# A tile's product with the values one step later in the two causal attentions of a decoder kernel

## The reference, cut to what matters

```python
scores = scale * einsum('bhqd,bhkd->bhqk', q, k)      # 2048 x 2048
scores = where(tril, scores, -inf)
out = einsum('bhqk,bhkd->bhqd', softmax(scores), v)
out = concat_heads(out) @ Wo.T + bo
x = layernorm(x + out)
```

## Time and profile before

| | |
|---|---|
| median of 3 runs | 2865.86 us (2857.93 to 2866.38) |
| the profiled execution | 2858.85 us |
| its span, first to last instruction | 2857.1 us |
| TensorE busy | 2657.4 us, 93% |
| VectorE busy | 2143.4 us, 75% |
| ScalarE busy | 1802.5 us, 63% |
| GpSimd busy | 533.8 us, 19% |
| mean granted TensorE clock | 0.963 |

### The profile page before, as it was taken

How to read it: one execution, slowest core, us unless ns; L and a number is a source line. 1 busy time by engine, 2 the same in 40 slices (tenths; PEclk the granted TensorE clock), 3 DMA queues, 4 the chain that set the end, 5 groups by cost and what they waited for, 6 DMA issues and landing times. The chain is left out here.

```text
span 2857.1 us, 93546 instructions
## 1 busy us (share of the span) xinstructions
PE 2657.4 (93%) x39187; PEld 1001.4 (35%) x39187; DVE 2143.4 (75%) x5870; ACT 1802.5 (63%) x2158; POOL 533.8 (19%) x742
## 2 busy tenths in 40 slices
PE   4999999999999999948999998999999999999997
PEld 1623333432222222324222224662222222266664
DVE  7689999479999999485899994139999999551115
ACT  2288888627777777733888886233888888822222
POOL 0078782030000000002222113212000000003330
PEclk8899999979999999978999999997999999999999
DMA  3456652241111110202111112010122221121112
GB/s 101 123 116 158 140 130 75 71 150 26 28 28 27 27 29 18 74 13 88 40 43 43 44 47 89 0 65 26 46 64 56 56 57 35 39 95 39 44 44 89
DMA packets 122804, 177.27 MB, mean 62 GB/s; under 512 B 38835, under 2 KB 89918, under 8 KB 122128
## 3 DMA queue, kind: packets, MB, share of 16 engines
q1 hardware_dynamic: 103344, 124.55, 16.5%
q0 software_dynamic: 13568, 46.17, 5.9%
q10 hardware_dynamic: 5472, 0.56, 0.2%
HBM read 131.75 MB, written 31.96 MB: 57 GB/s over the span
## 5 line engine op out<-in xcount | busy, mean ns | idle before, releaser
L811 DVE TENSOR_REDUCE mpart<-ps 128x1 f32<-128x512 f32 x1536 | 978.9, 683 | 77.2 <-PE ps L598 73.8
L598 PE MATMUL ps<-stack 48*32 48x512 f16 (+4 forms) x13312 | 939.5, 349 | 41.6 <-DVE mpart L811 12.8
L523 ACT ACTIVATE xT<-ps,exp_scale 128x1024 f32<-128x1024 f32 (+3 forms) x800 | 785.1, 1028 | 215.6 <-PE ps L619 107.0
L523 ACT ACTIVATE cn<-ps,exp_scale 128x1024 f32<-128x1024 f32 (+4 forms) x800 | 733.2, 959 | 155.2 <-PE ps L619 73.8
L619 PE MATMUL ps<-stack 50*32 50x512 f16 (+3 forms) x11648 | 761.3, 371 | 32.2 <-ACT xT L523 24.3
L598 PEld LDWEIGHTS ps<-stack 48*32 48x32 f16 x13312 | 276.5, 90 | 986.4 <-DVE mpart L811 515.1
L804 DVE CUSTOM_DVE_ANT_0 scrap<-ps,arena 128x512 bf16<-128x512 f32 x768 | 490.1, 686 | 40.7 <-PE ps L598 37.3
L668 PE MATMUL ps<-xT,vall 128*17 128x512 f32 (+4 forms) x3648 | 412.5, 512 | 2.6 <-POOL xT L482 1.7
L668 PE MATMUL ps<-cn,vall 128*17 128x512 f32 (+3 forms) x3392 | 408.4, 501 | 1.2 <-ACT cn L523 1.0
L619 PEld LDWEIGHTS ps<-stack 50*32 50x32 f16 x11648 | 202.2, 90 | 190.9 <-ACT xT L523 96.0
L788 DVE CUSTOM_DVE_ANT_0 scrap<-ps,scrap 128x128 bf16<-128x128 f32 (+3 forms) x512 | 247.3, 484 | 14.3 <-PE ps L598 8.9
(11 more groups left out here) (293 smaller groups left out, 2778.9 us busy)
## 6 DMA issues: line engine op xcount, KB each, us to landing
stack<-q_parts SPq DMA_DIRECT2D x384, 64.0 KB, 3.2
stack<-k_parts SPq DMA_DIRECT2D x192, 64.0 KB, 3.3
wbuf<-in_maskT POOLq DMA_DIRECT2D x48, 256.0 KB, 4.7
arena<-in_moe_w SPq DMA_DIRECT2D x19, 512.0 KB, 4.8
stack<-k_parts SPq DMA_DIRECT2D x192, 50.0 KB, 2.4
stack<-sums_inverse SPq DMA_DIRECT2D x16, 512.0 KB, 6.0
parts<-osb SPq DMA_DIRECT2D x240, 32.0 KB
wbuf<-in_mask POOLq DMA_DIRECT2D x16, 401.0 KB, 4.3
```

What stands on the lines that cost most here:

```text
L523: nc.scalar.activation(e.prob[tile % P_SLOTS][0:rows, half * HALF + first:(half + 1) * HALF], S_PS(g)[0:rows, first:HALF], ACT.Exp, scale= ...
L598: last = nc.tensor.matmul(bank[quarter(j), i * w:i * w + w], qs[b][rows, at:at + 32], ks[b][rows, a:a + w], start=True, stop=True)
L811: nc.vector.tensor_reduce(dst, src, AX, ALU.max).then_inc(unit_used, 1)
```

## The change

In the causal attentions the product of the tile that is complete with slot n moves from step n to step n+1, behind that step's scores and first units; the product of a head's last tile moves into step 0 of the next head, and that of the very last tile behind the loop. ScalarE's copy of the last head's output moves from behind the exponential of slot 1 to behind that of slot 2. The cross-attentions keep their order. No instruction is added or removed.

```diff
@@ units and slots
-    wide = not causal
+    wide, late_product = not causal, causal
@@ ScalarE, behind the exponential
-                        if n == 1 and h:
+                        if n == (2 if late_product else 1) and h:
                             copy_out(h - 1)
@@ TensorE, in step n of head h, behind the scores and the first units
-                        if slots[n][5]:
+                        if not late_product and slots[n][5]:
                             product(h, n)
+                        elif late_product and n and slots[n - 1][5]:
+                            product(h, n - 1)
+                        elif late_product and n == 0 and h:
+                            product(h - 1, ns - 1)
                         for u in now[middle:]:
                             unit(turned, u)
+                if late_product:
+                    product(H - 1, ns - 1)
                 pe.wait_ge(o_weights_in, 16 * NC)
```

## The result

The change made the kernel slower. The median of four runs is 2907.99 us (2906.55 to 2915.11) against 2861.89 us (2856.52 to 2866.38) in four runs of the kernel before: ratio 1.0175, with a 95% interval of 1.0161 to 1.0188. (The two profiled executions give 1.0175 too, the two medians alone 1.0161.) The profiled execution took 2908.75 us with a span of 2907.0 us, 49.9 more than the span before, at the same mean clock (0.962 against 0.963). The prediction said 2912.0.

The account below looks back on a forecast made before the run. VectorE was taken to set the pace in steps 1 to about 15, TensorE from 16 to the next head's step 0. 14.5 x (1.65 + 1.83) = 50.5 us on 2858.85 gave 2909, taken as 2912; range 2868 to 2937.

Parts of the forecast that it names:

- The ring of three banks: Steps 2 to 12: VectorE's three queued units run out before the next after a product (1.90 us); net 1.0 per head.
- overlap of 0.09: On VectorE, one maximum overlaps the next by 0.09 us, so lateness of 0.36 is printed as 0.27 idle.
- The sum per head: Middle and end of a causal head together: 1.65 us more in layer 0, 1.83 in layer 1.
- The total: Both causal attentions: 14.5 heads x (1.65 + 1.83) = 50.5 us more, nearly all on the path setting the end.
- The bounds: Loss over both causal stages: at least 18 us from the surest terms (1.2 per pair of heads), at most 66.
- absorbed case: VectorE's 1.5 us idle at the head boundary takes up the middle's added idle: no change, say 2863 us; chance 0.13.
- The end of a head: Slots 15 to 21 replace 16 to 22 before the next head's scores: 0.44 us, plus about 0.2 in layer 0.
- ScalarE's 0.3 in layer 1: Tile 5's product delays slot 15's scores, whose exponential releases slot 17's; ScalarE has 0.32 idle, needs some 0.6: 0.3 more.
- Before the exponentials of slots 6, 8, 10 and 12 ScalarE no longer waits.: Sign in even steps: scores no longer stand behind a product (0.52 at slot 12); said to give nothing.
- The copy: Step 2: done 0.1 to 0.4 us before tile 0's product may start; bound -0 to +0.3 per head.
- Balance: TensorE reaches products before the ring is full, VectorE's queue covers 1.90: about 0.9 us per head faster, 2833; chance 0.11.
- Half: The middle costs as worked out, but TensorE recovers 0.44 and 0.3: 33 us slower, 2892; within the 0.76 for slower.

Follow-up runs that it names:

- the end alone late: The kernel before with only the products of slots 16 to 23 one step late, copy in its old place: 1.0014.
- the mended kernels: Units 27, 31, 35 two places later: in the kernel after, 1.0095; in the kernel before with products 1-13, 20-23 and copy late, 1.0032.

## Why the prediction was right

Direction, size and the main mechanism were right. Two smaller statements, on ScalarE and on the copy, and one of the sums for the bounds were wrong; that the total fits to 0.8 us is in part luck.

- **The ring of three banks.** The prediction worked out a need of 1.90 us against VectorE's queue. In layer 0 it gave a lateness of 0.47, 0.36 and 0.46 in steps 4, 6 and 8, which by its own overlap of 0.09 would be printed as 0.38, 0.27 and 0.37: measured 0.41, 0.27 and 0.37. In step 12 it gave 0.2 (0.11 printed): 0.26 before unit 3 in the head shown; other heads have between 0 and 0.26 there, some with 0.24 to 0.30 before unit 6 instead. For layer 1 it gave 0.47, 0.60 and 0.25 in steps 6, 8 and 10, printed 0.38, 0.51 and 0.16: measured 0.41, 0.50 and 0.16. The ties of 0.10 to 0.12 in step 2 and in layer 1's step 4 are not printed. Turning the order of the units alone took away half of the loss (1.0175 to 1.0095) or made a similar one in the old kernel (1.0074), so this is shown, not only argued.
- **The sum per head.** From the second to the fifteenth turning of the maxima there are 13 heads. They run from 161.9 to 479.3 us in layer 0 before and from 161.7 to 500.0 after, in layer 1 from 1380.7 to 1694.6 and from 1405.7 to 1743.0. A head grows from 24.42 to 26.02 us in layer 0, 1.60 where 1.65 was predicted, and from 24.15 to 25.95 in layer 1, 1.80 where 1.83 was predicted. In the most regular heads of layer 0 it is only 1.49 (24.36 to 25.85); the kernel after has several longer ones, of 26.0 to 26.3 us, among them those with the idle before unit 6. The head's end is 0.57 of the predicted 0.64, which leaves 1.0 for the middle, as predicted.
- **The total.** Predicted were 50.5 us, 3.48 for each of 14.5 pairs of heads; measured were 22.7 and 27.0, 49.7 together. The 13 heads in between carry 44.2 of them. The first and the last interval grew by 0.6 and 1.3 us in layer 0 and by 2.4 and 1.2 in layer 1, 5.5 together, where the sum has 1.5 pairs of heads, 5.2. The prediction had no reason for this size at the edges of a stage, so that they fit is luck.
- **The bounds.** The lower one was added up wrongly: 0.47 + 0.36 - 0.6 + 0.44 is 0.67 and 0.47 + 0.60 - 0.5 + 0.44 is 1.01, so 1.7 per pair of heads and 24 us, and not 1.2 and 18. The range's lower end was taken from the absorbed case and doesn't hang on it.
- **The end of a head.** Predicted: tile 7's product in, tile 14's out, 0.44, and 0.2 for unit 9's wait. Measured: 0.35 up to the scores of slot 20 and 0.22 behind them. The 0.22 is the exchange of product widths and is there by itself with the end alone late. The 0.35 comes with the product of tile 7. A free step 16 gives nothing back (2.26 before, and 2.26 with the end alone late), so it starts from what was already a wait. How the 0.35 divides between the product's length and the 0.23 that the scores of slot 18 wait for ScalarE isn't shown.
- **ScalarE's 0.3 in layer 1.** Predicted as the exponential of slot 15 releasing the scores of slot 17; VectorE's idle of 0.33 before unit 2 is there. In the mended kernels it is 0.64, and it goes once the products of slots 11 and 13 come in their own steps. Right.
- **"Before the exponentials of slots 6, 8, 10 and 12 ScalarE no longer waits."** True, but not the whole: its waits moved to the odd slots, with 0.59 to 0.81 at slots 7, 9, 11 and 15, and the conclusion that this side is free was wrong. With the ring mended, scores that wait for exponentials are a part of what is left in 1.0118 (units late too), 1.0095 and 1.0032. The step of the working that failed, though the forecast didn't hang on it, is to take ScalarE's waits as idle time of an engine that isn't the bound: units stand behind scores on TensorE, so a late exponential is a late unit.
- **The copy.** Priced at -0 to +0.3 with "done before the product may start". As placed by the change it costs nothing visible. But the two halves of the edit aren't independent: a late copy with early products costs 1.1% and an early copy with late products adds 0.5%, of which about two thirds and somewhat under half stand in heads at full clock.
- **The rivals.** Absorbed: the idle at the head's end (0.51 and 0.99; 1.49) is unchanged to 0.01 us, so it takes up nothing. Balance: VectorE's queue doesn't cover the product. Half: the end of the head gives back nothing. The clock has hardly a part in it: the stretches shown have 1.00, and the mean is 1.00 from 150 to 500 us and 0.99 from 1370 to 1730 us.

Four comparisons put the parts side by side: the last four products late, -0.53%; the four before them late, +0.67% (1.0014 against 0.9947); the first seven late with the units mended, +0.85% (1.0032 against 0.9947); the narrow units in the product's queue, +0.80% (1.0175 against 1.0095). Together +1.79%, measured 1.75%. They were taken on several chips and need not add up, and slot 15's product by itself wasn't tried. But the traces say the same in us per head, between the turnings of the maxima as above: -0.29, +0.53, +0.38 and +0.98 in layer 0, together 1.60 (measured 1.60), and -0.45, +0.68, +0.84 and +0.74 in layer 1, together 1.81 (measured 1.80). No large part is missing.

## What to carry to other kernels

When an in-order engine feeds another through a small ring of buffers, a long operation on it belongs where the consumer's queue is longest in time, not in number: add up the durations of the buffers ahead and compare them with the wait, the operation and the start of the next one. An order of feeding work that looks arbitrary (which of the tiles is the narrow one) can then be worth as much as the place of the operation. And when moving something one step, divide the move: here the same edit was a gain for the last four products, which puts one product less ahead of the next head's first scores, and a loss in each other group that was tried. Last, look at more than one head before sizing a term: with the copy late alone the head shown had 1.70 us of idle where its neighbours have 1.00, since the clock had fallen in it.

## What the runs showed of the hardware

The clock was not on my list. The kernel before runs both causal stages at a mean granted clock of 1.00 (2.4 GHz). With the copy late and the products early the means are 0.98 and 0.97. Tile 0's product had waited 0.66 us for the copy in the turn shown, and took 1.52 instead of 1.05; with the copy early and the products late a 4 us stretch had 0.58, and the product in it took 1.91. Such a stretch reaches VectorE as idle (1.47 instead of 0.32) and makes the head some 1.1 us longer. It stands in nine of 28 heads with the copy late alone, in five with the first eight products late, in two with the copy early, and in none of the kernels before and after. (The head at the start of layer 1's stage is left out; the clock is below 1.00 there in all five.)

A longer wait for the copy doesn't decide it. With the copy late alone the product at 1457.00 waits the same 0.66 us as the one at 1481.82 and takes its 1.05 at full clock. And with the first eight products late, tile 0's product in the slow stretch (1496.18, 1.86 us) has no printed wait, and TensorE's waits in the 3 us ahead of it (0.20, 0.38, 0.20) are those of an undisturbed head. What decides it stays open.
